# How GpSimd spaces its row gathers in the first edge pass of a graph network kernel

## The reference

```python
msg_s = (s_n @ Ws_src)[src] + (s_n @ Ws_dst)[dst]
msg_v = einsum('ncx,cd->ndx', v_n, Wv_src)[src] + einsum('ncx,cd->ndx', v_n, Wv_dst)[dst]
w1 = rbf @ W_rbf
m1_s, m1_v = _cg_tp(msg_s, msg_v, y0, y1, *w1)     # products with the edge's harmonics
a = leaky(m1_s @ W_alpha) . alpha_dot              # logits of a softmax by target
val_s, val_v = m1_s @ Ws_val, einsum('ecx,cd->edx', m1_v, Wv_val)
val_v = val_v * sigmoid(val_s @ Wg)                # the gate
m2_s, m2_v = _cg_tp(sigmoid(val_s), val_v, y0, y1, w2...)
h = m2_s @ Ws_vlin, einsum(m2_v, Wv_vlin)
agg = segment_sum(softmax(a) * h, dst)
```

## Time and profile before

| | |
|---|---|
| time, median of 3 runs | 9591.08 us (9548.35 to 9623.26) |
| the profiled execution | 9599.6 us, its span 9597.3 us |
| busy share of the span | PE 81%, PEld 64%, DVE 71%, ACT 54%, POOL 52% |
| first edge pass, from the first to the last sum of gathered rows | 238.7 to 5921.3 us |
| granted TensorE clock, mean | 0.836 |

### The profile page before, as it was taken

One profiled execution on the slowest core, in us unless ns is written; L12 is line 12 of the kernel. 1 busy time (PEld: TensorE's weight loads), 2 busy tenths in 40 slices (PEclk: granted clock), 3 DMA queues, 4 the chain that ended last, 5 costly groups with the idle time before them and its releaser, 6 DMA issues. The chain is left out here.

```text
span 9597.3 us, 196058 instructions
## 1 busy us (share of the span) xinstructions
PE 7798.3 (81%) x43972; PEld 6155.8 (64%) x43973; DVE 6800.5 (71%) x16742; ACT 5176.7 (54%) x16950; POOL 5019.7 (52%) x5222
## 2 busy tenths in 40 slices
PE   5788888888878888888888887898788887887778
PEld 3677777777767777767777776897444444444446
DVE  7667667767767666676677777787777776776677
ACT  5455555555545555555555554113666666666665
POOL 1555555555545555555555553784366665565650
PEclk7777777777777777787777878999899999999999
DMA  7333222222222222222222222677444443443435
GB/s 242 74 77 76 78 75 77 77 77 78 78 68 78 77 75 75 76 79 75 74 78 78 77 76 59 220 223 153 116 113 114 111 112 104 110 112 107 111 105 174
DMA packets 971876, 968.06 MB, mean 101 GB/s; under 512 B 452750, under 2 KB 788750, under 8 KB 971662
## 3 DMA queue, kind: packets, MB, share of 16 engines
q0 software_dynamic: 225792, 385.65, 16.4%
q1 hardware_dynamic: 512032, 346.40, 13.0%
q10 hardware_dynamic: 233936, 234.90, 7.4%
HBM read 677.57 MB, written 288.65 MB: 101 GB/s over the span
## 5 line engine op out<-in xcount | busy, mean ns | idle before, releaser
L745 POOL DMA_INDIRECT e_g_dst<-table_dst,e_idx x1568 | 1495.5, 954 | 1695.2 <-ACT logits L898 1324.1
L784 PE MATMUL e_ps_t<-ident,e_m 128*128 128x128 f32 (+1 forms) x7840 | 1499.7, 334 | 687.0 <-issue 307.2
L745 POOL DMA_INDIRECT e_g_src<-table_src,e_idx x1568 | 1497.4, 955 | 988.6 <-issue 608.2
L2021 POOL DMA_INDIRECT f_e<-table,f_src x1568 | 1492.0, 952 | 980.8 <-issue 521.8
L784 PEld LDWEIGHTS e_ps_t<-ident,e_m 128*128 128x128 f32 (+1 forms) x7840 | 1128.0, 170 | 891.6 <-issue 598.8
L2078 PE MATMUL f_ps_a<-sums 128*128 128x384 f32 x3936 | 1514.7, 531 | 1.5 <-DVE sums L2178 1.5
L877 ACT ACTIVATE e_m1t<-e_ps_t 128x512 f32<-128x512 f32 (+1 forms) x1176 | 688.0, 598 | 950.2 <-remote 393.6
L2078 PEld LDWEIGHTS f_ps_a<-sums 128*128 128x128 f32 x3936 | 763.3, 204 | 569.7 <-issue 216.7
L2067 PE MATMUL f_ps_w<-f_w,f_hidden 64*128 64x192 f32 x3936 | 491.9, 372 | 494.1 <-DVE sums L2178 242.3
L1004 DVE TENSOR_TENSOR e_vy<-e_msg,e_ps_w 128x384 f32<-128x384 f32 x392 | 216.7, 553 | 817.4 <-ACT e_ps_w L957 513.2
L896 ACT ACTIVATE e_ps_v<-e_ps_v 128x128 f32<-128x128 f32 x392 | 102.7, 262 | 1284.4 <-remote 726.7
(11 more groups left out here) (268 smaller groups left out, 17900.8 us busy)
## 6 DMA issues: line engine op xcount, KB each, us to landing
edge_values<-e_h ACTq DMA_DIRECT2D x392, 330.0 KB
r_h<-edge_values SPq DMA_DIRECT2D x196, 660.0 KB, 4.0
sums<-sums ACTq DMA_DIRECT2D x492, 192.0 KB
e_g_src<-table_src,e_idx POOLq DMA_INDIRECT x1568
e_g_dst<-table_dst,e_idx POOLq DMA_INDIRECT x1568
f_e<-table,f_src POOLq DMA_INDIRECT x1568
f_rbf<-basis SPq DMA_DIRECT2D x492, 48.0 KB
basis<-t_part SPq DMA_DIRECT2D x42, 448.0 KB, 3.1
```

Source lines behind the costliest of these rows:

```text
L745: pool.indirect_dma_start(out=into[:, r, t, :], out_offset=None, in_=table, in_offset=bass.IndirectOffsetOnAxis(ap=idx[:, r, c:c + 1], axi ...
L784: last = nc.tensor.transpose(ps_t[bank][0:channels, t * P:(t + 1) * P], rows(t), ident[:])
L2021: pool.indirect_dma_start(out=rows_of_units[:, (place * RING + r) * T + t, :], out_offset=None, in_=table, in_offset=bass.IndirectOffsetOn ...
```

## The change

The semaphore of landed gathers, one for each place, becomes three: `from_src` and `from_dst` count the first three gathers of a run, and `fourths` counts the fourth of both runs. GpSimd waits for three landed gathers of the run before ahead of every run of four: ahead of the target rows for the source rows of the same group, ahead of the source rows for the target rows of the group before. The wait for `gated` goes. SP and VectorE, which waited for all eight gathers on one semaphore, wait on three.

```diff
@@ SP
-                    wait(sp, gathered[r], i * 32 * T)
+                    wait(sp, from_src[r], i * 16 * (T - 1))
+                    sp.sem_inc(issued, 1)
+                    wait(sp, from_dst[r], i * 16 * (T - 1))
+                    sp.sem_inc(issued, 1)
+                    wait(sp, fourths[r], i * 32)
                     sp.dma_start(idx[:, r, :], idx_d[u]).then_inc(idx_in[r], 16)
@@ GpSimd
                 wait(pool, first, (u - RING) * FIRST + MSG if not isinstance(u, int) or u >= RING else 0)
+                if not isinstance(u, int) or u > 0:
+                    pool.wait_ge(from_dst[(r - 1) % RING], (i + 1 if r else i) * 16 * (T - 1))
                 pool.sem_inc(issued, 1)
-                for side, (table, into) in enumerate(((table_src, g_src), (table_dst, g_dst))):
-                    if side == 1 and (not isinstance(u, int) or u >= RING):
-                        wait(pool, gated, u - RING)
+                for side, (table, into, landed) in enumerate(((table_src, g_src, from_src),
+                                                              (table_dst, g_dst, from_dst))):
+                    if side == 1:
+                        pool.wait_ge(from_src[r], (i + 1) * 16 * (T - 1))
                         pool.sem_inc(issued, 1)
                     for t in range(T):
                         c = side * T + t
                         pool.indirect_dma_start(
                             ...
-                        ).then_inc(gathered[r], 16)
+                        ).then_inc(landed[r] if t < T - 1 else fourths[r], 16)
@@ VectorE
-                dve.wait_ge(gathered[r], (i + 1) * 32 * T)
+                dve.wait_ge(from_src[r], (i + 1) * 16 * (T - 1))
+                dve.wait_ge(from_dst[r], (i + 1) * 16 * (T - 1))
+                dve.wait_ge(fourths[r], (i + 1) * 32)
```

More of the change, by code:

```diff
@@ L625, in edges @@
                                                     sem("ones_set"))
-        idx_in, y_in, rbf_in, gathered = ([sem(f"{n}{r}") for r in range(RING)]
-                                          for n in ("idx_in", "y_in", "rbf_in", "gathered"))
+        idx_in, y_in, rbf_in, from_src, from_dst, fourths = ([sem(f"{n}{r}") for r in range(RING)]
+                                          for n in ("idx_in", "y_in", "rbf_in", "from_src", "from_dst", "fourths"))
         stored = [sem(f"stored{r}") for r in range(2)]
```

## The result

The changed kernel takes 9748.01 us (median of 9729.56, 9748.01 and 9778.21) where the kernel before took 9591.08: a ratio of 1.017, 95% interval 1.010 to 1.025. A gain of 6.5% was forecast, a loss of 1.7% came. The profiled execution took 9729.56 us, with a span of 9727.8 us.

A forecast was written before the change was run, and what follows sets the result against it. No engine is full; runs of gathers hold back TensorE's results. 391 x 12.75 + 66 = 5051 us for the first pass against 5682.6, or -631 us from the profiled 9599.6, gave 8970 us, range 8830 to 9350.

The forecast's parts named there:

- The bound: First pass, 14.53 us a group: no engine full, no wait for gathered rows; gathers being issued hold back TensorE's results.
- Removing it as such is worth nothing: GpSimd's wait for the gate, 1324.1 us in all, is not on the path, so removing it gains nothing by itself.
- The pause of 2.2 us and the last target gather at 9.7 us: GpSimd pauses 2.2 us between source and target runs; last target gather comes 9.7 us behind the first source gather.
- about 2.1 us behind the fourth source gather: Sign of being right: ScalarE's gate stays this far behind the fourth source gather.
- The long holds: Runs of gathers without pause, after a late second gather about 33 times, disappear; they cost 8 us each, 264 us.
- The first rival: Only the long holds go, ordinary groups stay between 12.75 and 15.05 us: -264 us, 9340 us; chance 0.13.
- The added waits at nothing: Added wait instructions of VectorE, SP and GpSimd cost 0, within bounds of 0 to 0.3 us a group, 0 to 117 us.
- The steady state closes on itself: 12.75 us: Target run ends 3.05 us ahead of the next source run, so every ordinary group of the first pass takes 12.75 us.
- the 66 us I had put down for late gathers: Late second gather stays, 33 times, each making the second group of its pair late by 2 us: 66 us.
- The third rival, slower: Pause too short, TensorE held until behind the target run, 18.7 us a group: +1630 us, 11,230 us; chance 0.07.
- My own sign of failure, a pause of 1.9 us or less: Prediction fails if GpSimd's pause between runs comes out at 1.9 us or less, or at over 3.
- The other phases stay: Everything outside the first pass keeps its time; only the first pass changes, by -631 us.

The follow-up runs named there:

- e2: Kernel before with only GpSimd's wait for ScalarE's gate taken away, no pauses, so eight gathers form one run; 10659 us, ratio 1.110.
- e1: Changed kernel with GpSimd's wait for ScalarE's gate put back ahead of the target rows, both pauses kept; 9246 us, ratio 0.964.
- e3: Kernel before with only the semaphores and waits split as in the change, gate's wait kept, no pauses; 9579 us, ratio 0.998.
- e13: Changed kernel with TensorE computing the four matmuls of the heads three times over; 10147 us, ratio 1.054.
- e9: Changed kernel, pauses kept, with the target rows also waiting for ScalarE's copy of the heads; 9302 us, ratio 0.978.
- e12: Changed kernel with the source run halved: runs of two, two and four, each behind its pause, no gate's wait; 9127 us, ratio 0.948.
- e14: Changed kernel, same pauses, with GpSimd also waiting for TensorE's finished mix ahead of the target rows; 9571 us, ratio 0.959.
- e15: Changed kernel with runs of two, two and four, and a wait for TensorE's finished mix ahead of the target rows; 9322 us, ratio 0.934.
- e8: Changed kernel with the gate's wait put back and the source run halved: runs of two, two and four; 9071 us, ratio 0.954.

## Why the prediction was wrong, point by point

**The bound: right.** No engine is full, VectorE never waits for gathered rows, and the gathers act on the others through TensorE.

**"Removing it as such is worth nothing": wrong.** The gate's wait was not on the path, but it kept the target run behind the mix of the group that was due. Taken away alone it costs 11% (e2), taken away beside the pauses 5.5% (1.017 against 0.964).

**The pause of 2.2 us and the last target gather at 9.7 us: right.** 2.04 us (median 2.10), and 1827.90 - 1818.35 = 9.55 us. The gate "about 2.1 us behind the fourth source gather" was not kept: 3.43 us there.

**The long holds: right that they go, and about their size.** But for a few at the start, all runs are of four. The low-clock groups of 18.94 us before were mostly theirs. The first rival had 264 us for them alone; e1 gains 5682.6 - 5342.8 = 340 us of the first pass.

**The added waits at nothing: right**, 0.998 (e3).

**"The steady state closes on itself: 12.75 us": the step that failed.** I asked of the target run only how far its end lies from the next source run, 3.05 us, and took that as sufficient, since that was what told two neighbours apart. Nothing checked its beginning. It now begins at 8.5 us, 2.04 us behind the fourth source gather, just when the mix held by the source run is due to be handed over (1.98 us behind it in e1, 2.15 in my rows). In 73 of 378 groups the gate came 0.5 to 1.5 us into the target run instead, TensorE idled, and 64 times the next group ran at the 1.2 GHz level. In numbers: the groups at a higher clock came at 13.37 us, (13.37 - 12.75) x 391 = 242 us over the forecast, and the low ones add 150 x (17.56 - 13.37) = 628 us; less the 66 us I had put down for late gathers, 804 us, which is the distance from -631 to +171 within 3 us. The low groups of the kernel before added 68 x (18.94 - 13.53) = 368 us already. This sum tells low from other groups; it doesn't prove that the clock is the cause of all the 628. My rows had the warning: 0.50 of clock and 10.11 us of waiting at 2675 were read as the length of the hold, not as its price through the clock.

**The third rival, slower: right in sign and in its condition, wrong in its price.** It was "decided where the pause falls under the 2.1 us that a result takes to come", and with a median pause of 2.10 us that is where the change landed. But in those 73 groups the gate is not held until the target run's end, 11.85 us behind the first source gather; at 1825.54 it is 7.19 us behind it. My own sign of failure, a pause of 1.9 us or less, was set too low. The rival had a chance of 0.07, and its 11,230 us are far from 9748; e2, with one long run, is where something like it can be seen.

**The other phases stay: right to 39 us**, 3637.2 against 3676.0 behind the last sum. Over e1 to e13, which don't differ there, this part varied from 3556.4 (e9) to 3746.8 us (e12), in e14 and e15 on the slower chip it was 3843.1 and 3875.6. I found no cause, and it is why periods of the first pass stand beside the times.

**The page "SBUF — State Buffer" of the Trainium skill**, section "SBUF: two separate sides", by which a DMA doesn't slow a compute op, gave 9600 us. Kernels that differ in little but when GpSimd issues the same gathers ran from 0.934 to 1.110 of the time. No run shows a compute op itself slowed; what comes late is the hand-over of TensorE's results, and I was wrong to let the page's rule stand for that.

What stays open: why a run of gathers holds TensorE's results at all, and whether it is GpSimd's issuing or the transfers that follow, which no run separates; what brings about the 86 low groups without a late gate; and how the loss divides between late results and low clock, since the two came together except where GpSimd set the pace.

## What to carry to other kernels

A wait that is on nobody's path may still be what spaces two kinds of traffic: before you remove it, lay its begin and its end against everything that is handed over in that stretch, not only against the next event that the forecast is about. Where long and short groups exist side by side, split them by granted clock first, and price a stall with what it does to the clock of the group behind it. Pauses between short runs of gathers (two, two, four here) gained 4.6 to 6.6% in a kernel in which no wait for gathers was visible, and with them the gathering engine came to set the pace. Before two variants are compared, look whether the wait in which they differ ever ends a wait at all: in e8 it ended 0.6 us.

## What the runs showed of the hardware

A run of GpSimd's indirect gathers delays results of TensorE to the other engines, and the delay grows with the run: in the commonest case until 2.5 to 3.0, 4.0 to 4.5 and 5.5 to 6.0 us behind the first gather for runs of two, three and four with gathers 1.25 us apart. In a run of eight some results get out in between (8.54 us in), so it isn't a lock held until the end. The late second gather, idle for 1.88 us ahead of it, which came every 170.9 us in the first pass before, came there only once with the change and once in e1; I had expected it to stay. The pauses are not what ended it: in e3, which has none and only splits the waits, it came once too, near 409 us. There long runs went on all the same, and 69 groups had a low clock, as many as before.
